# Keys and values ahead of the queries in a two-layer graph network kernel, with two smaller moves

## The chip, the cores and the metric

The kernel runs on one core of a Trainium2 chip. The metric is the device time of one execution in microseconds, lower is better.

## The reference

A graph of 3125 nodes with 128 features and 103125 edges (sources `src`, targets `dst`, sorted by target). Cut to what matters:

```python
# layer 0: graph convolution
deg  = segment_sum(1, src);  norm = rsqrt(deg)[src] * rsqrt(deg)[dst]
x = layernorm(x + segment_sum(norm * (x @ weight)[src], dst) + bias)
# layer 1: message passing with edge weights from two small networks
w = silu(edge64 @ rad_w0 + rad_b0) @ rad_w1 + rad_b1
w = w + silu(edge32 @ sph_w0 + sph_b0) @ sph_w1 + sph_b1
q = (x @ wq)[dst];  k = (x @ wk)[src];  v = (x @ wv)[src]
alpha = (q * w * k).sum(per head of 16) / sqrt(16) * edge_weight
x = layernorm(x + segment_sum(alpha * v, dst) / 16)
```

## The kernel before, in words

The edges are cut into 202 groups of 512 (four tiles of 128). Each engine has its own program, written by hand, and all order between engines comes from semaphores that the code names. Four stages follow one another.

**Prologue.** VectorE counts degrees with one-hot rows, scales the node rows (L1211), splits the first layer's weights of the edge networks into a high and a low part (L1218, L1222), then checks with two reductions (L1227, L1228) that the sorted order of the targets fits the windows. The checked values come from GpSimd: differences (L620, L624 to L635), then a copy and two scalings (L639 to L641), counted on the semaphore `s_set`. From the check follow the two pass counts, one for each sweep; every engine reads them from SBUF into a register (L416), and each is 1 for these inputs. TensorE waits for the split weights through `s_pre` (L916).

**Sweep one** runs over all groups: GpSimd gathers scaled node rows for half of them, the others are counted into dense blocks, TensorE sums both into `acc` (a column for each node) and also computes the edge weights of a quarter of the groups, which are stored to HBM.

**The gap.** 25 blocks of 128 nodes go in 7 chunks of 4 (the last has one). For a chunk c, in this order of engines: TensorE multiplies `acc` with the layer's weights (`convolve`, L1032); VectorE adds the rows, takes statistics; ScalarE takes the root (`root`, L815) and normalises (`scaled`, L821); TensorE transposes (L1042); ScalarE copies the transposes to `x_t`, two chunk buffers (`copy_transposes`, L829); `project` on TensorE makes queries (L1051), then keys and values (L1058). ScalarE copies keys and values out (`copy_kv`, L849) and, with VectorE, splits the queries into three bf16 parts: `q_hi` (L836), the rest (L1445), `q_mid` (L841), the low part (L1448). `q_rest` is one buffer, `q_parts` has four chunk slots, reused when the stores of the chunk four earlier have landed (L835). All of that is one software pipeline, with one loop on each engine. SyncE's loop (L531 to L543) stores a chunk's keys and values (L534), then waits for its low part and stores three query parts (L538; for chunk 1 three more, L542), then takes the next chunk. GpSimd adds a bias to the node rows (L691), clears `acc` (L694), and waits until all keys and values have landed (L696).

**Sweep two** runs over all 202 groups, in 50 steps of four and a last one of two. GpSimd issues four indirect gathers of keys and values for each group (L657, a ring of eight group slots, reused after the message of the group eight earlier). SyncE loads the gather's indices (L461, after the gathers of four pairs before have landed, L460), rows, queries (L506, the first only after all query stores, L552), edge features (L451, L453) and stored weights. ScalarE and VectorE split features, TensorE runs the edge network (L930, L932, L948), expands queries (L1082) and sums messages (L958). VectorE multiplies keys with queries (L1487), then with weights (L1499), sums heads (L1504), makes the message (L1519), in an order written out by hand in `sweep2`. At the end the second layer norm and the stores to `out`.

Of the kernel before, what the change touches and what calls it, by code (L numbers as in the profile page):

```python
# [19 lines left out]
P = 128  # L20
# [114 lines left out]
def build(nc, x, x_pad, src_idx, src_e, dst_e, dst_row, dst_first, cut_e, rad_t, sph_t, w_l0, b_l0, rad_w0, rad_b0,  # L135
# [24 lines left out]
    with ExitStack() as ctx:  # L160
# [132 lines left out]
        x_t, to = part(count, 0, 2 * CHUNK * P)  # L293
        x_t = x_t.rearrange("p (k f) -> p k f", k=2)
        q_rest, to = part(count, to, CHUNK * D)
# [139 lines left out]
        def _(sp):  # L435
# [95 lines left out]
            for c in range(CHUNKS):  # L531
# [3 lines left out]
                             kv_out[:, c % 4, 0:n, :]).then_inc(s_kvt[c % 4], 16)  # L535
                sp.wait_ge(s_lo, c + 1)
# [53 lines left out]
        def _(pool):  # L590
# [56 lines left out]
            assert v == SET.all, v  # L647

            pool.wait_ge(s_pre, PRE.passes)
            n_pass1, n_pass2 = passes(pool, 1), passes(pool, 2)  # L650
# [38 lines left out]
            for c in range(CHUNKS):  # L689
                own = nodes[:, blocks(c)[0]:blocks(c)[-1] + 1, :]  # L690
                pool.tensor_tensor(own, own, b_l0_sb[:, :].unsqueeze(1).to_broadcast([P, len(blocks(c)), D]),  # L691
                                   ALU.add).then_inc(s_biased, 1)
            pool.wait_ge(s_conv, CHUNKS)
# [10 lines left out]
        def _(act):  # L704
# [44 lines left out]
            n_pass1, n_pass2 = passes(act, 1), passes(act, 2)  # L749
# [74 lines left out]
            def copy_transposes(c):  # L824
                act.wait_ge(s_tr, c + 1)
                if c >= 2:
                    act.wait_ge(s_proj, blocks(c - 2)[-1] + 1)
                cols = slice(0, len(blocks(c)) * P)
                act.activation(x_t[:, c % 2, cols], bank[2 + c % 2][:, cols], ACT.Copy).then_inc(s_trc, 1)  # L829
# [8 lines left out]
            def q_mid(c):  # L838
                cols = slice(0, len(blocks(c)) * D)
                act.wait_ge(s_rest, c + 1)  # L840
                act.activation(q_parts[:, c % 4, 1, cols], q_rest[:, cols], ACT.Copy).then_inc(s_mid, 1)  # L841
# [25 lines left out]

# [8 lines left out]

            with act.Fori(0, n_pass2) as p:
# [12 lines left out]
        def _(pe):  # L890
# [25 lines left out]
            pe.wait_ge(s_pre, PRE.w0)  # L916
# [128 lines left out]
            def project(c):  # L1045
                pe.wait_ge(s_trc, c + 1)
                if c >= 2:
                    pe.wait_ge(s_rest, c - 1)
                for b in blocks(c):
                    at = b % CHUNK * P  # L1050
                    mm = pe.matmul(bank[4 + c % 2][:, at:at + D], x_t[:, c % 2, at:at + P], wqkv[:, 0:D],  # L1051
                                   start=True, stop=True, skip_group_check=True)
                mm.then_inc(s_projq, 1)
                for b in blocks(c):
                    if b >= 4 and b % 2 == 0:
                        pe.wait_ge(s_projc, b // 2 - 1)
                    at, to = b % CHUNK * P, b % 2 * 2 * D
                    pe.matmul(bank[6 + b // 2 % 2][:, to:to + 2 * D], x_t[:, c % 2, at:at + P], wqkv[:, D:3 * D],  # L1058
                              start=True, stop=True, skip_group_check=True).then_inc(s_proj, 1)
# [3 lines left out]
            for c in range(CHUNKS):  # L1063
# [81 lines left out]
        def _(dve):  # L1145
# [99 lines left out]
            dve.wait_ge(s_set, SET.all)  # L1245
# [193 lines left out]
            def split_q(c):  # L1439
# [3 lines left out]
                if c >= 1:  # L1443
                    dve.wait_ge(s_lo, c)
                dve.tensor_tensor(q_rest[:, cols], bank[4 + c % 2][:, cols], q_parts[:, c % 4, 0, cols],  # L1445
                                  ALU.subtract).then_inc(s_rest, 1)
# [248 lines left out]
```

## Time and profile before

| | us |
|---|---|
| median of 3 runs | 1775.34 (1770.6 to 1778.68) |
| the profiled execution's own time | 1772.56 |
| its span in the profile | 1770.7 |
| TensorE busy | 1571.4 (89%) |
| VectorE busy | 1379.2 (78%) |
| GpSimd busy | 1298.8 (73%) |
| ScalarE busy | 924.5 (52%) |

Sweep one begins at about 84 us of the span and ends at about 621; the gap reaches to 667, sweep two to about 1748. Busy shares are averages over these stages, so a change in one stage has to be read in the rows of that stage. PE is TensorE, DVE is VectorE, ACT is ScalarE, POOL is GpSimd, SP is SyncE; a q behind the name is the engine's queue, which also issues DMAs.

### The profile page before, as it was taken

To read this page: it belongs to the slowest core of one execution; us is meant where nothing else is said; L and a number is where in the kernel's file an instruction comes from. 1 tells how busy PE (TensorE), PEld (TensorE's weight loads), DVE (VectorE), ACT (ScalarE), POOL (GpSimd) and SP (SyncE) were. 2 spreads that over 40 slices of the span, in tenths; PEclk is the share of its full clock that TensorE was granted. 3 is DMA by queue.
4 is the path that set the end of the run, shared out by engine and by line. 5 is a ranking of instruction groups with operands and counts; after the bars stand their busy time and mean duration, and the time that the engine had idled before them with its cause. 6 is when DMAs were issued, how large, how long until landed. Compare 5 with 4: busy or idle time off the path is not lost.

```text
span 1770.7 us, 45707 instructions
## 1 busy us (share of the span) xinstructions
PE 1571.4 (89%) x12986; PEld 1454.2 (82%) x12986; DVE 1379.2 (78%) x3869; ACT 924.5 (52%) x1399; POOL 1298.8 (73%) x1249
## 2 busy tenths in 40 slices
PE   3389999899899978999999999999999999999995
PEld 2278888888888866889988898989898898888984
DVE  8986777777777566887887788887888777888886
ACT  1144555554555374555555555555555555555563
POOL 8777777777777627777777777777777777777771
PEclk9999999999999988999999999999999999999997
DMA  3133333333333266666666666666666666666663
GB/s 100 43 104 101 107 105 99 106 105 99 106 105 100 77 166 160 178 177 175 181 178 172 175 174 176 179 176 184 178 176 179 177 175 172 172 178 176 180 181 105
DMA packets 177657, 259.26 MB, mean 146 GB/s; under 512 B 80694, under 2 KB 91757, under 8 KB 177436
## 3 DMA queue, kind: packets, MB, share of 16 engines
q0 software_dynamic: 51840, 132.72, 27.8%
q1 hardware_dynamic: 120008, 120.99, 24.4%
q10 hardware_dynamic: 5716, 4.55, 0.9%
q8 instruction: 30, 0.49, 0.1%
q14 instruction: 63, 0.52, 0.1%
HBM read 235.32 MB, written 22.79 MB: 146 GB/s over the span
## 4 chain that ended last, share of the span: by engine, by line
POOL 43%; issue 18%; DVE 14%; PE 14%; DVEq 4%; DMA 3%; POOLq 1%; SPq 1%; ACT 1%; ACTq 1%
POOL arena L657 40%; PE bank L948 5%; PE bank L991 4%; DVE count L1342 4%; POOL rel L620 3%; DVE xsplit L1309 2%; DVE key_hot L1330 2%; PE bank L958 2%; DVE low_hot L1329 2%; DVEq L1315 1%; DMA arena<-kv_d,idx 1%; DMA xraw<-in_sph_t 1%; DVEq L1342 1%; PE bank L930 1%; POOLq L674 1%
## 5 line engine op out<-in xcount | busy, mean ns | idle before, releaser
L657 POOL DMA_INDIRECT arena<-kv_d,idx x808 | 823.3, 1019 | 264.4 <-issue 262.3
L948 PEld LDWEIGHTS bank<-w,hid 128*128 128x128 f32 x6464 | 779.9, 193 | 24.0 <-ACT hid L773 1.5
L948 PE MATMUL bank<-w,hid 128*128 128x128 f32 x6464 | 788.7, 277 | 0.0
L773 ACT ACTIVATE hid<-bank,b 128x512 f32<-128x512 f32 x808 | 495.6, 683 | 308.3 <-PE bank L932 301.7
L657 POOL DMA_INDIRECT arena<-xs_d,idx x408 | 394.5, 967 | 139.8 <-issue 121.0
L930 PE MATMUL bank<-xsplit,w_hi 128*128 128x512 f32 x808 | 344.8, 437 | 79.1 <-ACT hid L773 54.5
L765 ACT ACTIVATE xsplit<-xraw 64x1024 fp32r<-64x1024 f32 x202 | 212.4, 1052 | 239.0 <-DMA xraw<-in_sph_t 224.1
L1309 DVE TENSOR_TENSOR xsplit<-xraw,xsplit 64x256 fp32r<-64x256 f32 x808 | 287.9, 413 | 6.6 <-ACT xsplit L765 0.2
L930 PEld LDWEIGHTS bank<-xsplit,w_hi 128*128 128x128 f32 x808 | 154.7, 191 | 113.2 <-ACT hid L773 63.4
L1342 DVE TENSOR_TENSOR count<-count,bank 128x200 f32 x400 | 144.5, 361 | 124.8 <-issue 57.9
L958 PE MATMUL bank<-onehot,late 128*128 128x126 f32 x1616 | 215.0, 281 | 6.3 <-DVE late L1519 4.5
L958 PEld LDWEIGHTS bank<-onehot,late 128*128 128x128 f32 x1616 | 193.2, 192 | 8.6 <-DVE late L1519 6.4
L1478 DVE TENSOR_SCALAR late<-late,iota_part 126x512 bf16<-126x512 bf16 x202 | 73.6, 365 | 118.8 <-PE bank L1082 102.6
L932 PE MATMUL bank<-xsplit,w_lo 128*128 128x512 f32 x404 | 160.4, 397 | 0.0
L1487 DVE TENSOR_TENSOR late<-arena,bank 128x512 f32<-128x512 f32 x202 | 137.3, 680 | 14.2 <-DMA arena<-kv_d,idx 10.2
L1499 DVE TENSOR_TENSOR late<-late,bank 128x512 f32<-128x512 f32 x151 | 102.9, 681 | 57.9 <-PE bank L948 52.8
L1519 DVE TENSOR_TENSOR late<-arena,alpha 128x512 f32<-128x512 f32 x202 | 138.6, 686 | 3.6 <-DVE alpha L1511 1.5
L1504 DVE TENSOR_REDUCE red<-late 128x32 f32<-128x512 f32 x202 | 136.8, 677 | 0.0
L791 ACT ACTIVATE w_sb<-bank 128x512 f32<-128x512 f32 x51 | 30.5, 597 | 189.6 <-PE bank L948 189.4
L757 ACT ACTIVATE bank<-b_full 128x512 f32<-128x512 f32 x199 | 118.6, 596 | 1.6
L1330 DVE TENSOR_SCALAR key_hot<-iota_key,key 128x200 bf16<-128x200 bf16 x400 | 113.4, 285 | 0.0
L1329 DVE TENSOR_SCALAR low_hot<-iota_key,low_f 128x128 bf16<-128x128 bf16 x400 | 107.6, 270 | 0.2
(144 smaller groups left out, 1310.6 us busy)
## 6 DMA issues: line engine op xcount, KB each, us to landing
late<-relrow_d SPq DMA_DIRECT2D x103, 256.0 KB
xraw<-in_rad_t SPq DMA_DIRECT2D x205, 128.0 KB
xraw<-in_sph_t SPq DMA_DIRECT2D x410, 64.0 KB
w_sb<-w_d SPq DMA_DIRECT2D x52, 256.0 KB, 4.0
w_d<-w_sb SPq DMA_DIRECT2D x51, 256.0 KB
arena<-kv_d,idx POOLq DMA_INDIRECT x808
arena<-xs_d,idx POOLq DMA_INDIRECT x408
qwin<-q_d SPq DMA_DIRECT2D x101, 31.5 KB
```

Of the source, the lines that this page charges most:

```text
L657: pool.indirect_dma_start(gath[:, k, t * width:(t + 1) * width], None, table, bass.IndirectOffsetOnAxis(ap=idx[:, pair.slot(4), j * TILES ...
L765: act.activation(xsplit[0:RAD, s.slot(2), :, :], xraw[:, k, :, :], ACT.Copy).then_inc(mlp.s_hi, 1)
L773: act.activation(hid[:, s.slot(2), c, :], hid_ps[s.sub(4, c, 4 * s.total).slot(len(hid_ps))][:, :], ACT.Silu, bias=b0[:, c:c + 1]).then_in ...
L930: mm = pe.matmul(to, w0_hi[:, m, cols], xsplit[:, b, m, :], start=True, stop=(m == 1))
L932: mm = pe.matmul(to, w0_lo[:, m, cols], xsplit[:, b, m, :], start=False, stop=True)
L948: mm = pe.matmul(w_ps[:, t * D:(t + 1) * D], hid[:, b, c, t * P:(t + 1) * P], w1[:, c, :], start=False, stop=(c == 3), skip_group_check=True)
L958: return pe.matmul(bank[7][:, at:at + 3 * WIN], rows, onehot[:, b, first:first + 3, :].rearrange("p t n -> p (t n)"), start=(k == 0), stop ...
L1309: last = dve.tensor_tensor(xsplit[RAD:P, b, m, half], xraw[:, k, m, half], xsplit[0:RAD, b, m, half].bitcast(F32), ALU.subtract)
L1329: dve.tensor_scalar(low_hot[:, t, :], iota_key[:, 0:LO], low_f[:, ds(col, 1)], None, ALU.is_equal)
L1330: last = dve.tensor_scalar(key_hot[:, t, :], iota_key[:, :], key[:, ds(col, 1)], None, ALU.is_equal)
L1342: dve.tensor_tensor(here, here, count_ps[j % 2][:, t * KEYS:(t + 1) * KEYS].rearrange("p (h w) -> p h w", h=NB), ALU.add).then_inc(s_add, 1)
L1519: dve.tensor_tensor(msg[:, j, :, :].rearrange("p t (h d) -> p t h d", d=HD), kv(g)[:, :, 1, :].rearrange("p t (h d) -> p t h d", d=HD), a, ...
```

## The change

1. The weights' split moves from VectorE (`pre`, counted on `s_pre`) to GpSimd (`step`, counted on `s_set`), behind GpSimd's copies for the spans. TensorE waits for `s_set`.
2. GpSimd and ScalarE read the first sweep's pass count at the old place; the second's only after the bias additions (GpSimd) and right before sweep two (ScalarE).
3. In the gap, the pipeline loop carries keys and values alone, for all chunks. `x_t` now holds all 25 blocks. The queries get a loop of their own behind it, on TensorE, ScalarE, VectorE and SyncE. `q_rest` gets two slots, in the memory of `prod`. SyncE stores all keys and values before any query part. TensorE waits for the last `s_rest` before sweep two.

The three subtractions, the sizes of the stores and every matrix product stay as they were.

```diff
-        x_t, to = part(count, 0, 2 * CHUNK * P)
-        x_t = x_t.rearrange("p (k f) -> p k f", k=2)
-        q_rest, to = part(count, to, CHUNK * D)
+        x_t, to = part(count, 0, NB * P)
+        q_rest = prod
...
                 sp.dma_start(kv_d[rows, :].rearrange("(b p) f -> p b f", p=P),
                              kv_out[:, c % 4, 0:n, :]).then_inc(s_kvt[c % 4], 16)
+
+            for c in range(CHUNKS):
+                n, rows = len(blocks(c)), slice(blocks(c)[0] * P, (blocks(c)[-1] + 1) * P)
                 sp.wait_ge(s_lo, c + 1)
...
-            assert v == SET.all, v
+            assert v == SET.spans, v
+            pool.wait_ge(s_whi, 1)
+            v = step(pool.tensor_tensor(w0_lo[:, :, :], w0_raw[:, :, :], w0_hi[:, :, :].bitcast(F32), ALU.subtract))
+            step_wait(v)
+            for j in (1, 3):
+                own = slice(j * SPH, (j + 1) * SPH)
+                v = step(pool.tensor_tensor(w0_hi[own, 1, :], w0_raw[own, 1, :], w0_hi[own, 1, :].bitcast(F32), ALU.subtract))
+            assert v == SET.w0, v
+            step_wait(v)
 
             pool.wait_ge(s_pre, PRE.passes)
-            n_pass1, n_pass2 = passes(pool, 1), passes(pool, 2)
+            n_pass1 = passes(pool, 1)
...
                                    ALU.add).then_inc(s_biased, 1)
+            n_pass2 = passes(pool, 2)
             pool.wait_ge(s_conv, CHUNKS)
...
-            n_pass1, n_pass2 = passes(act, 1), passes(act, 2)
+            n_pass1 = passes(act, 1)
...
             def copy_transposes(c):
                 act.wait_ge(s_tr, c + 1)
-                if c >= 2:
-                    act.wait_ge(s_proj, blocks(c - 2)[-1] + 1)
...
                 if c < CHUNKS:
                     copy_transposes(c)
-                if c >= 1:
-                    q_hi(c - 1)
                 if c + 1 < CHUNKS:
                     scaled(c + 1, s_shift, s_norm)
                 if c >= 1:
                     copy_kv(c - 1)
-                    q_mid(c - 1)
                 if c + 2 < CHUNKS:
                     root(c + 2, s_var, s_std)
+            for c in range(CHUNKS + 1):
+                if c < CHUNKS:
+                    q_hi(c)
+                if c >= 1:
+                    q_mid(c - 1)
...
+            n_pass2 = passes(act, 2)
             with act.Fori(0, n_pass2) as p:
...
-            pe.wait_ge(s_pre, PRE.w0)
+            pe.wait_ge(s_set, SET.w0)
...
                 if c >= 1:
-                    project(c - 1)
-            project(CHUNKS - 1)
+                    project_kv(c - 1)
+            project_kv(CHUNKS - 1)
+            for c in range(CHUNKS):
+                project_q(c)
             pe.wait_ge(s_projc, (NB + 1) // 2)
+            pe.wait_ge(s_rest, CHUNKS)
...
-            dve.wait_ge(s_whi, 1)
-            v = pre(dve.tensor_tensor(w0_lo[:, :, :], w0_raw[:, :, :], w0_hi[:, :, :].bitcast(F32), ALU.subtract))
-            pre_wait(v)
-            for j in (1, 3):
-                own = slice(j * SPH, (j + 1) * SPH)
-                v = pre(dve.tensor_tensor(w0_hi[own, 1, :], w0_raw[own, 1, :], w0_hi[own, 1, :].bitcast(F32), ALU.subtract))
-            assert v == PRE.w0, v
...
-                if c >= 1:
-                    split_q(c - 1)
+            for c in range(CHUNKS + 1):
+                if c < CHUNKS:
+                    rest_of_q(c)
+                if c >= 1:
+                    low_of_q(c - 1)
```

`project_kv` and `project_q` are the two halves of `project`, and `rest_of_q` and `low_of_q` those of `split_q`, with their waits; `rest_of_q(c)` waits for the low part of chunk c - 2.

## Rows read from the trace of the kernel before

**Rows 1.** The page's costliest groups: busy, mean ns of one | idle before.

```profile
L657 POOL DMA_INDIRECT arena<-kv_d,idx x808 | 823.3, 1019 | 264.4 <-issue 262.3
```

**Rows 2.** Timeline of the gap's end: start us, us, engine, line, operation.

```profile
660.92 0.39 ACT L849 ACTIVATE arena<-bank 128x256 f32<-128x256 f32 x1
...
663.68 0.54 SPq L534 DMA_DIRECT2D kv_d<-arena  x1
...
667.38 1.05 POOL L657 DMA_INDIRECT arena<-kv_d,idx  x1 [18.48 <-issue]
```

**Rows 3.** Waits of GpSimd, 700 to 1760 us: total us, times, longest us.

```profile
POOL arena L657 <- issue: 236.5, 776, 0.3
```

**Rows 4.** Waits of SyncE's queue, 700 to 1760 us.

```profile
SPq L460 <- DMA arena<-kv_d,idx: 431.9, 95, 6.3
```

**Rows 5.** Timeline of VectorE in sweep two, first products of two steps.

```profile
808.21 0.68 DVE L1487 TENSOR_TENSOR late<-arena,bank 128x512 f32<-128x512 f32 x1
...
828.11 0.68 DVE L1487 TENSOR_TENSOR late<-arena,bank 128x512 f32<-128x512 f32 x1
```

**Rows 6.** Windows of sweep two: PE, PEld, DVE, ACT, POOL busy (instructions), PEclk, DMA, GB/s.

```profile
700.00:900.00 200.00, 189.47 (x1535) 179.54 (x1532) 164.51 (x384) 111.24 (x170) 153.93 (x152) 0.99 0.66 179
...
760.00:780.00 20.00, 20.00 (x166) 19.03 (x165) 17.34 (x41) 12.01 (x20) 15.43 (x16) 1.00 0.64 169
```

**Rows 7.** Timeline of ScalarE in the gap.

```profile
639.74 0.59 ACT L829 ACTIVATE count<-bank 128x512 f32<-128x512 f32 x1
...
640.21 0.60 ACT L836 ACTIVATE count<-bank 128x512 bf16<-128x512 f32 x1
...
643.77 0.63 ACT L841 ACTIVATE count<-count 128x512 bf16<-128x512 f32 x1 [0.37 <-DVE count L1445]
...
658.03 0.27 ACT L829 ACTIVATE count<-bank 128x128 f32<-128x128 f32 x1
```

**Rows 8.** Timeline of TensorE in the gap.

```profile
641.61 1.05 PE L1032 MATMUL bank<-w_l_sb,acc 128*128 128x128 f32 x8
...
642.94 1.06 PE L1051 MATMUL bank<-wqkv,count 128*128 128x128 f32 x8
...
643.83 1.89 PE L1058 MATMUL bank<-wqkv,count 128*128 128x256 f32 x8
```

**Rows 9.** Timeline of VectorE: a query subtraction, first product, first message.

```profile
643.05 0.69 DVE L1445 TENSOR_TENSOR count<-bank,count 128x512 f32<-128x512 f32 x1
...
674.15 0.69 DVE L1487 TENSOR_TENSOR late<-arena,bank 128x512 f32<-128x512 f32 x1 [6.57 <-DMA arena<-kv_d,idx]
...
680.92 0.69 DVE L1519 TENSOR_TENSOR late<-arena,alpha 128x512 f32<-128x512 f32 x1
```

**Rows 10.** The query stores' line: issue ns min/median/max, first and last start.

```profile
L538 SPq DMA_DIRECT2D q_d<-count x21: 372/454/989, 640.5 to 665.2; - x21
```

**Rows 11.** DMA view, 655 to 672 us: GB/s in 40 slices; stores, KB, us to landing.

```profile
GB/s 301 318 225 211 214 217 28 0 202 347 316 343 224 206 216 222 298 347 311 324 236 214 215 215 300 227 97 0 0 0 0 0 55 175 154 11 213 180 0 193
...
kv_d<-arena SPq DMA_DIRECT2D x2, 512.0 KB, 3.3
```

**Rows 12.** Timeline of the prologue, and TensorE's first layer.

```profile
19.68 51.54 POOL L620 TENSOR_TENSOR rel<-dst_f,base_f 128x808 f32<-128x808 f32 x1 [7.65 <-ACT dst_f L725]
...
71.19 1.02 POOL L624 TENSOR_TENSOR near<-dst_f,tile_f 128x400 f32<-128x400 f32 x1
...
75.16 2.07 POOL L640 TENSOR_SCALAR arena<-near 128x400 f32<-128x400 f32 x1
76.08 1.00 DVE L1218 TENSOR_TENSOR w_lo<-w_raw,w_hi 128x512 fp32r<-128x512 f32 x1
...
77.31 1.29 POOL L641 TENSOR_SCALAR arena<-coff 128x400 f32<-128x400 f32 x1
...
95.33 0.79 PE L930 MATMUL bank<-xsplit,w_hi 128*128 128x512 f32 x1 [12.12 <-DVE xsplit L1309]
```

**Rows 13.** The pass count's read on GpSimd's queue: ns min/median/max.

```profile
L416 POOLq TENSOR_LOAD <-passes_i x2: 312/410/507, 83.7 to 84.5; - x2
```

More of the change, by code:

```diff
@@ L825, in copy_transposes @@
                 act.wait_ge(s_tr, c + 1)
-                if c >= 2:
-                    act.wait_ge(s_proj, blocks(c - 2)[-1] + 1)
                 cols = slice(0, len(blocks(c)) * P)
-                act.activation(x_t[:, c % 2, cols], bank[2 + c % 2][:, cols], ACT.Copy).then_inc(s_trc, 1)
+                own = slice(blocks(c)[0] * P, (blocks(c)[-1] + 1) * P)
+                act.activation(x_t[:, own], bank[2 + c % 2][:, cols], ACT.Copy).then_inc(s_trc, 1)
             def q_hi(c):
@@ L840, in q_mid @@
                 act.wait_ge(s_rest, c + 1)
-                act.activation(q_parts[:, c % 4, 1, cols], q_rest[:, cols], ACT.Copy).then_inc(s_mid, 1)
+                act.activation(q_parts[:, c % 4, 1, cols], q_rest[:, c % 2, cols], ACT.Copy).then_inc(s_mid, 1)
             def copy_kv(c):
@@ L1043, in transpose, with project_kv, project_q @@
                 mm.then_inc(s_tr, 1)
-            def project(c):
+            def project_kv(c):
                 pe.wait_ge(s_trc, c + 1)
+                for b in blocks(c):
+                    if b >= 4 and b % 2 == 0:
+                        pe.wait_ge(s_projc, b // 2 - 1)
+                    to = b % 2 * 2 * D
+                    pe.matmul(bank[6 + b // 2 % 2][:, to:to + 2 * D], x_t[:, b * P:(b + 1) * P], wqkv[:, D:3 * D],
+                              start=True, stop=True, skip_group_check=True).then_inc(s_proj, 1)
+            def project_q(c):
                 if c >= 2:
@@ L1050, in project @@
                     at = b % CHUNK * P
-                    mm = pe.matmul(bank[4 + c % 2][:, at:at + D], x_t[:, c % 2, at:at + P], wqkv[:, 0:D],
+                    mm = pe.matmul(bank[4 + c % 2][:, at:at + D], x_t[:, b * P:(b + 1) * P], wqkv[:, 0:D],
                                    start=True, stop=True, skip_group_check=True)
                 mm.then_inc(s_projq, 1)
[L1054 to L1059, printed above, removed]
             convolve(0)
@@ L1242, in _ @@
             assert v == PRE.passes, v
-            dve.wait_ge(s_set, SET.all)
+            dve.wait_ge(s_set, SET.spans)
             dve.wait_ge(s_cast, CAST.all)
@@ L1437, in scale_and_shift, with rest_of_q, low_of_q @@
                                          op0=ALU.mult, op1=ALU.mult).then_inc(s_shift, 1)
-            def split_q(c):
+            def rest_of_q(c):
                 cols = slice(0, len(blocks(c)) * D)
                 dve.wait_ge(s_hi, c + 1)
-                if c >= 1:
-                    dve.wait_ge(s_lo, c)
-                dve.tensor_tensor(q_rest[:, cols], bank[4 + c % 2][:, cols], q_parts[:, c % 4, 0, cols],
+                if c >= 2:
+                    dve.wait_ge(s_lo, c - 1)
+                dve.tensor_tensor(q_rest[:, c % 2, cols], bank[4 + c % 2][:, cols], q_parts[:, c % 4, 0, cols],
                                   ALU.subtract).then_inc(s_rest, 1)
+            def low_of_q(c):
+                cols = slice(0, len(blocks(c)) * D)
                 dve.wait_ge(s_mid, c + 1)
-                dve.tensor_tensor(q_parts[:, c % 4, 2, cols], q_rest[:, cols], q_parts[:, c % 4, 1, cols],
+                dve.tensor_tensor(q_parts[:, c % 4, 2, cols], q_rest[:, c % 2, cols], q_parts[:, c % 4, 1, cols],
                                   ALU.subtract).then_inc(s_lo, 1)
@@ L1625 @@
     xs = 14
-    w0 = 18
-    viol = 22
-    passes = 25
+    viol = 19
+    passes = 22
 class SET:
     rel = 8
-    all = 11
+    spans = 11
+    w0 = 14
 class CAST:
```

## The prediction

> **What bounds the kernel now.** I read the page's costliest groups first, looking for the instruction that fills an engine without a gap. It is GpSimd's second gather: 808 of them, 1.019 us each, with 264.4 us of idle in front that is nearly all "issue" [rows 1]. 18.48 of that lies ahead of the first one, at 667.38 [rows 2]; the rest is (264.4 - 18.5) / 807 = 0.305 apiece. So a gather takes 1.019 + 0.305 = 1.324 us and a step of four groups (16 gathers) 21.2. GpSimd's waits over the second sweep say that no gap was longer than 0.3 us: it never waited for anybody [rows 3]. So the end moves with the **start of the first gather**, as long as the others keep up.
>
> Do the others follow GpSimd or set its pace? SyncE's waits tell: 95 of its index loads, of one for each of 101 pairs, stood until a gather had landed [rows 4], and the features that feed TensorE are queued behind them. When the others fall behind they make it up: two first products of a step (L1487) stand at 808.21 and 828.11, a step of 19.9 us [rows 5]. The windows show TensorE busy 20.00 of 20 us with 166 instructions done, against 1535 in 200 us on average [rows 6]. A step holds 1535 / 200 x 21.2 = 163 of them, so it can run in 163 / 166 x 20 = 19.6 us. TensorE looks full and has over 1 us in each step to give.
>
> **The gap between the sweeps** (622 to 667). ScalarE's copies of transposes (L829) stand at 639.74 for chunk 2 and 658.03 for chunk 6: a turn is 18.29 / 4 = 4.57 us, and the one idle of a turn is 0.37 [rows 7]. ScalarE sets this loop. Two items of its turn, 0.60 (L836) and 0.63 (L841), serve the queries alone. On TensorE a turn has a convolution of 1.05, four transposes (half its instructions, 0.53), 1.06 of queries and 1.89 of keys and values [rows 8]: 4.53.
>
> **Keys and values first.** Without the queries ScalarE's turn is 4.57 - 1.23 = 3.34 us and TensorE's 4.53 - 1.06 = 3.47; VectorE loses two subtractions of 0.69 [rows 9]. I take 3.5. Copy 2 comes at 638.7, 1 us sooner than now, since scaling no longer waits for a query product; copies 3 to 5 follow at 3.5 each, 649.2. The tail has no convolution left: chunk 4's and 5's keys and values and those of chunk 6's single block (1.89 + 1.89 + 0.5 on TensorE, their copies beside and behind, with the last transposes between) put the last copy's end at 654.9. Now it is 660.92 + 0.39 = 661.31 [rows 2].
>
> SyncE's queue counts too. The last store of keys and values was ready at 661.31 and issued at 663.68, behind query stores [rows 2]: 2.4 us. In the new order only chunk 5's store stands ahead. Issue at 655.2, 8.5 us sooner. The first gather began 3.7 us after that issue [rows 2]. The 512 KB store right before it needs 3.3 to land [rows 11], so I give back 0.5: first gather at 659.4, **8.0 us sooner**. Ends: 5 (the three engines wait for one another, a turn near 4.2) and 10 (a turn of 3.2, since operations overlap a little).
>
> **Queries in a loop of their own.** They start when ScalarE has copied the last keys, 654.9, and end later than now. Per chunk ScalarE does 0.60 + 0.63 and VectorE 0.69 + 0.69 [rows 7, 9]; seven chunks at 1.4 give 665. But a part buffer comes free only when the stores of the chunk four earlier have landed, and SyncE issues 24 stores (21, and 3 for the rows past the end) at 0.45 each [rows 10], 11 us, from 657.8 on: 669, some 3 more to land, 672. Their data runs at 201 to 234 GB/s where keys and values reach 302 to 350 [rows 11]: 2.4 MB in 11 us, and the gathers (131 KB each 1.32 us) want a third of that time, up to 677. The last query store is now issued at 665.2 [rows 10] and is in by 668. So the queries are 4 to 9 us late, and the first product of sweep two, which at 674.15 still waited 6.57 for its gather [rows 9], comes at 674 to 679. **Priced at nothing**: the cover is the distance between a gather and its use. A slot is gathered again eight groups (42.4 us) on; the first message ended at 681.6 [rows 9], at most 687 afterwards, and is needed by 659.4 + 42.4 = 701.8. The lag of up to 5 + 8 = 13 us is worked off at 21.2 - 19.9 = 1.3 us a step, in ten of the fifty. Without that cover it costs the lateness itself, 0 to 5 us.
>
> **Weights on GpSimd.** VectorE's L1218 (1.00) and both L1222 go. VectorE then waited for GpSimd's L641, which ended at 78.60, so their own time is worth nothing. What counts is that GpSimd's two scalings ran beside them, 2.07 and 1.29 us, though L624 over the same 400 columns took 1.02 [rows 12]. At 1.02 each they end 1.3 sooner; part of L640 stands beside L1211, which stays, so I take **1.0 us sooner**, ends 0 and 1.8. VectorE's chain from there to the sweep carries it whole. The Trainium skill (SBUF — State Buffer, "Who interferes with whom") says that a VectorE operation with two SBUF inputs and a GpSimd one that reads SBUF shut each other out for the whole instruction, and that a VectorE reduction never does; L640 did end 0.15 after L1218, so the trace agrees. By that rule the estimate would be 1.8. The three subtractions cost GpSimd 512 x 2.55 ns + 2 x 0.65 = 2.6 us (2.55 ns a column, from L624), 78.3 to 81; TensorE needs them at 94, one before its 95.33 [rows 12], and GpSimd's next work is the first gather. Nothing.
>
> **Pass count read later.** A read is a load of 0.3 to 0.5 us on each engine's queue and some 0.2 after it [rows 13]. GpSimd's moves beside VectorE's statistics, at 630: nothing. ScalarE's moves in front of sweep two, +0.65, where the work waits for queries: nothing.
>
> **Sum**, against the profiled execution's 1772.56: -8.0 - 1.0 = 1763.6. It lies 2.8 us under the median of the runs shown, 1775.34; there the sum is **1766.3**, -0.51%. A measurement of this kernel tells about 0.5% (8.9 us) from no change, so the forecast stands on that line.
>
> **Rivals.**
> Half the gain (11%): the engines of the new loop wait for one another, a turn of 4.5; first gather 4 us sooner, -5, 1770.3. For it: three turns of nearly equal length. Against: ScalarE idles only 0.37 in a turn.
> The first weights held back (4%): GpSimd's L620 took 51.54 us for 808 columns while VectorE made 16-bit one-hots [rows 12]. If the new subtractions are held so until about 101, TensorE's first layer (95.33) starts 5.7 late: -8 + 5.7, 1773. Against: L640 and L641 got through beside VectorE.
> **Slower** (12%, of it 5% past the line): the queries decide. Place: first product of sweep two. If steps can't run under 21.2 us, the end moves with that product and not with the gather. At 679 that is +5 - 1, 1779; if buffers and shared transfers push it to 689, +15 - 1, 1789. It decides once the lag outlives the 50 steps, 13 / 50 = 0.26 a step, so at steps over 20.9. Against it: the 19.9 of [rows 5].
> More than forecast (8%): a turn of 3.2, nothing given back, 1.8 in front: -12, 1763.3.
>
> **Numbers.** The forecast has 65%; its spread of some 2 us either way and that of the runs put 42 of these past the line and 23 within. Faster 42 + 8 = 50%; within 23 + 11 + 4 + 7 = 45%; slower 5%. Range 1760.5 to 1772.5: -12 and -5 with the scatter of a median of runs (they lay 1770.6 to 1778.7) of some 2.5 beyond each.
>
> **What would show it.** L1227 1 us sooner; copies of transposes 3.5 apart; last store of keys and values issued near 655 and the first gather near 659, each less that 1 us; query stores in one block to about 669; first product at 674 to 679, then steps under 20.5 until the lag is back; and still no gap over 0.4 us between gathers. It is wrong if GpSimd waits for VectorE's messages.

## The result, and the profile after

| | before | after |
|---|---|---|
| median of 20 runs each, us | 1773.39 | 1769.15 (1761.77 to 1775.31) |
| ratio, 95% interval | 1 | 0.9971 (0.9958 to 0.9983) |
| the profiled execution, us | 1772.56 | 1775.31 |

The change makes the kernel 0.3% faster, some 5 us by the ratio, where 9 were forecast. The time lies in the range. One of the 20 runs of the kernel before took 2772.29 us; it hardly moves the median. The profiled execution of after is the slowest of its 20 runs. So the totals of the two pages must not be held against each other, and below a stage is read from three executions of the same gap (after, e1 and e10).

The page's costliest group, which answers to [rows 1]:

```profile
L667 POOL DMA_INDIRECT arena<-kv_d,idx x808 | 833.1, 1031 | 260.4 <-issue 257.3
```

The idle in front of the gathers is 4.0 us less than before, all of it at the first gather (14.46 us where it was 18.48). The mean gather is 12 ns longer, which over 808 is 9.8 us: in this execution more than the head start.

The gap between the sweeps, timeline of after (columns as in [rows 2]): ScalarE's copies of transposes (L839), then SyncE's last two stores of keys and values (L533), GpSimd's clear of the accumulator (L705) and the first gather (L667), and one small VectorE operation (L1424).

```profile
637.70 0.60 ACT L839 ACTIVATE count<-bank 128x512 f32<-128x512 f32 x1 [0.34 <-PE bank L1055]
640.78 0.59 ACT L839 ACTIVATE count<-bank 128x512 f32<-128x512 f32 x1
645.79 0.58 ACT L839 ACTIVATE count<-bank 128x512 f32<-128x512 f32 x1
648.92 0.58 ACT L839 ACTIVATE count<-bank 128x512 f32<-128x512 f32 x1
...
654.75 0.91 SPq L533 DMA_DIRECT2D kv_d<-arena  x2
...
642.74 2.88 POOL L705 MEMSET acc<- 128x3344 f32 x1 [13.11 <-PE bank L1045]
660.08 0.97 POOL L667 DMA_INDIRECT arena<-kv_d,idx  x1 [14.46 <-issue]
...
643.50 2.15 DVE L1424 TENSOR_SCALAR rstd<-meanvar 128x4 f32<-128x4 f32 x1
645.68 0.20 ACT L826 ACTIVATE rstd<-rstd 128x4 f32<-128x4 f32 x1 [1.74 <-DVE rstd L1424]
```

A turn is 3.1 us, except one of 5.0: copies at 640.78 and 645.79. VectorE's operation on four columns, elsewhere 0.17, took 2.15 and ended at 645.65, which is 0.03 after the end of GpSimd's clear (642.74 + 2.88 = 645.62). ScalarE's root stood 1.74 for it. The first gather begins 7.3 us sooner than in [rows 2].

The queries and the start of sweep two, timelines of SyncE's queue and VectorE:

```profile
671.86 1.01 SPq L540 DMA_DIRECT2D q_d<-count  x2
676.27 1.78 SPq L505 DMA_DIRECT2D qwin<-q_d  x2
...
679.27 0.69 DVE L1502 TENSOR_TENSOR late<-arena,bank 128x512 f32<-128x512 f32 x1 [4.77 <-PE bank L1100]
```

The last query store goes out at 672.4 and the first query load 3.9 us later. The first product stands 5.1 us after that of [rows 9], and it now waits for the expanded queries and not for its gather.

GpSimd's waits, 700 to 1760 us, and two windows (columns as in [rows 6]):

```profile
POOL arena L667 <- issue: 233.7, 767, 0.3
POOL arena L667 <- DVE late L1534: 3.0, 10, 0.3
```

```profile
660.00:680.00 20.00, 6.37 (x31) 4.39 (x30) 9.33 (x23) 11.60 (x17) 15.35 (x16) 0.64 0.88 216
700.00:900.00 200.00, 195.59 (x1616) 186.66 (x1615) 169.84 (x400) 119.57 (x180) 154.51 (x150) 1.00 0.67 180
```

Still no gap over 0.3 us, as in [rows 3]: GpSimd sets the end in both kernels. The engines behind it do 1616 matrix instructions in 200 us where [rows 6] has 1535, and VectorE is busy 169.84 instead of 164.51: they work the lag off. Their first step of four groups, from first product to first product, takes 27.0 us (26.6 in the kernel before), the next ones 19.5 to 19.7 each.

The prologue, timeline of after, answers to [rows 12]:

```profile
75.17 2.07 POOL L642 TENSOR_SCALAR arena<-near 128x400 f32<-128x400 f32 x1
77.31 1.21 POOL L643 TENSOR_SCALAR arena<-coff 128x400 f32<-128x400 f32 x1
...
78.56 1.83 DVE L1236 TENSOR_REDUCE small<-arena 128x1 f32<-128x1608 f32 x1 [2.40 <-POOL arena L643]
...
78.88 1.25 POOL L651 TENSOR_TENSOR w_lo<-w_raw,w_hi 128x512 fp32r<-128x512 f32 x1
80.21 1.52 POOL L655 TENSOR_TENSOR w_hi<-w_raw,w_hi 32x256 fp32r<-32x256 f32 x2
...
94.94 0.79 PE L943 MATMUL bank<-xsplit,w_hi 128*128 128x512 f32 x1 [11.79 <-DVE xsplit L1318]
```

VectorE's subtraction is gone from beside the two scalings, and they take 2.07 and 1.21 us as before (2.07 and 1.29).

### The profile page after: what moved, and what is told of

Read it like the earlier page. It is cut to its first block, busy times and chain, and to the rows that moved or that the text cites. A ratio compares the mean times of both kernels' runs of the same rounds, so it can differ in the third digit from the quotient of the medians.

```text
span 1773.5 us, 45704 instructions
## 1 busy us (share of the span) xinstructions
PE 1572.9 (89%) x12986; PEld 1456.7 (82%) x12986; DVE 1379.2 (78%) x3866; ACT 926.0 (52%) x1399; POOL 1310.4 (74%) x1252
## 4 chain that ended last, share of the span: by engine, by line
POOL 44%; issue 18%; PE 15%; DVE 14%; DVEq 4%; DMA 2%; POOLq 1%; ACTq 1%; SPq 1%; ACT 1%
POOL arena L667 40%; PE bank L961 5%; PE bank L1004 4%; DVE count L1351 4%; POOL rel L622 3%; DVE xsplit L1318 2%; DVE key_hot L1339 2%; DVE low_hot L1338 2%; PE bank L971 2%; DVEq L1324 1%; PE bank L943 1%; DVEq L1351 1%; POOLq L684 1%; DMA arena<-kv_d,idx 1%; DMA xraw<-in_sph_t 1%
## 5 line engine op out<-in xcount | busy, mean ns | idle before, releaser
L667 POOL DMA_INDIRECT arena<-kv_d,idx x808 | 833.1, 1031 | 260.4 <-issue 257.3
L667 POOL DMA_INDIRECT arena<-xs_d,idx x408 | 394.3, 966 | 136.9 <-issue 121.3
L1318 DVE TENSOR_TENSOR xsplit<-xraw,xsplit 64x256 fp32r<-64x256 f32 x808 | 287.6, 412 | 6.4
L1514 DVE TENSOR_TENSOR late<-late,bank 128x512 f32<-128x512 f32 x151 | 103.1, 683 | 56.3 <-PE bank L961 51.6
L1534 DVE TENSOR_TENSOR late<-arena,alpha 128x512 f32<-128x512 f32 x202 | 138.8, 687 | 3.6 <-DVE alpha L1526 1.9
```

Source lines behind the costliest of these rows:

```text
L667: pool.indirect_dma_start(gath[:, k, t * width:(t + 1) * width], None, table, bass.IndirectOffsetOnAxis(ap=idx[:, pair.slot(4), j * TILES ...
L1318: last = dve.tensor_tensor(xsplit[RAD:P, b, m, half], xraw[:, k, m, half], xsplit[0:RAD, b, m, half].bitcast(F32), ALU.subtract)
L1534: dve.tensor_tensor(msg[:, j, :, :].rearrange("p t (h d) -> p t h d", d=HD), kv(g)[:, :, 1, :].rearrange("p t (h d) -> p t h d", d=HD), a, ...
```

## The experiments

The kernels came in four sessions, each with its own runs of the kernel before (1772.83, 2555.86, 1772.33 and 2489.86 us). In the second and the fourth the granted clock of TensorE was 0.84 and 0.86 on the mean of every execution, instead of 0.98; these numbers are compared with one another alone.

### e1_gap_only and e2_front_only: one part of the change each

e1 is the changed kernel with the weights back on VectorE and both pass counts read early; e2 has those two moves, and the gap of the kernel before. Both cuts are against the changed kernel.

```diff
 e1:
-            n_pass1 = passes(act, 1)
+            n_pass1, n_pass2 = passes(act, 1), passes(act, 2)
...
-            pe.wait_ge(s_set, SET.w0)
+            pe.wait_ge(s_pre, PRE.w0)
 e2:
-                    project_kv(c - 1)
+                    project(c - 1)
```

> Only the gap is reordered (keys and values first, queries in their own loop); weights' split and pass counts as in the kernel before. Theory A (the end moves with the first gather, and the gap gave all of the gain): first gather near 660.4, last store of keys and values issued near 656, time 5 to 7 us under the kernel before. Rival (the front moves matter as I forecast, 1.0 us or more of the gain): at most 4 us under the kernel before.

> Only the weights' split on GpSimd and the later pass counts. Theory A: VectorE's first reduction starts only 0.1 us sooner because GpSimd's scaling there takes as long as before; TensorE's first layer 0.4 sooner; time 0 to 0.5 us under the kernel before, not to be told from no change. Rival (my forecast): 1.0 us or more sooner, first reduction at 77.6.

Measured: e1 1768.89 us, ratio 0.9983 (0.9966 to 0.9999), first gather at 659.43; e2 1772.70 us, ratio 0.9998 (0.9982 to 1.0013), first gather at 667.00, first reduction of the check at 78.55 (78.63 in the kernel before). So the gap's part carries the gain, and the two moves in front show none: 0.1 us by the medians of e2, and no difference within its interval. The gain of e1, 3.9 by the medians, is less than the 5 to 7 that its first theory gave and lies where its rival had it (at most 4), but the rival's reason, a gain in front, is what e2 does not show. In e2 the first layer of TensorE starts 0.41 us sooner (94.92 against 95.33 of [rows 12]).

### e3_gather_held: the first gather behind the query stores

The changed kernel, with one wait more on GpSimd ahead of the gathers:

```diff
+            for j in range(4):
+                pool.wait_ge(s_qt[j], 48 * (chunks_in(j, 4) + (j == 1)))
```

> The changed kernel, but GpSimd also waits until all query stores have landed before its first gather of sweep two. Theory A (the end follows the first gather one to one): first gather near 677, 17 us later than in the changed kernel, end 17 us later, about 12 us slower than the kernel before. Theory B (the first product decides and gathers are hidden): no more than 4 us over the changed kernel. Theory C (working off the lag makes gathers longer, about 4 us of the early start given back): end only 13 us later than in the changed kernel, because there is no lag to work off, with the gather stream back to about 1068 us.

Measured: 1779.35 us, ratio 1.0036 (1.0021 to 1.0051).

```profile
674.75 0.97 POOL L667 DMA_INDIRECT arena<-kv_d,idx  x1 [28.00 <-issue]
...
681.42 0.69 DVE L1504 TENSOR_TENSOR late<-arena,bank 128x512 f32<-128x512 f32 x1 [7.22 <-DMA arena<-kv_d,idx]
```

The first gather is 14.7 us later than in after, the first product only 2.2, and the median is 10.2 higher (10.5 above e1's, which stands beside the same runs of before). If the first product decided, it would be 2. So the end follows the gather. But nearly a third of the 14.7 did not arrive: these 4.5 us were owed to something that a late start doesn't have, as the third theory had it. Against e2, which starts late too, the gather is 7.75 us later and the median 6.7 higher. The gathers themselves tell where the rest went. GpSimd's groups by line, for gathers 65 to 128 (the second block of 64) of before, after and e3: busy, mean ns | idle before.

```profile
L657 POOL DMA_INDIRECT arena<-kv_d,idx x64 | 65.3, 1021 | 19.5 <-issue 19.5
```

```profile
L667 POOL DMA_INDIRECT arena<-kv_d,idx x62 | 66.3, 1069 | 18.9 <-issue 18.6 <-DVE late L1534 0.3
```

```profile
L667 POOL DMA_INDIRECT arena<-kv_d,idx x65 | 66.0, 1016 | 19.8 <-issue 19.5 <-DVE late L1536 0.3
```

And the windows of the same stretches, in the same order:

```profile
751.00:835.00 84.00, 78.64 (x634) 74.89 (x635) 66.89 (x158) 47.16 (x72) 64.71 (x64) 0.98 0.64 178
```

```profile
743.00:828.00 85.00, 85.00 (x708) 81.41 (x707) 72.84 (x170) 51.63 (x78) 66.15 (x62) 1.00 0.67 180
```

```profile
758.00:843.00 85.00, 76.65 (x618) 72.81 (x617) 64.48 (x151) 46.91 (x72) 65.23 (x65) 0.98 0.66 179
```

Where the others catch up, VectorE is busy 86% of the stretch instead of 80 and 76, and a gather takes 1.069 us instead of 1.021 and 1.016. In e1, e10 and e4, which start early too, it takes 1.065, 1.069 and 1.073; in e2, which starts late, 1.010. That is 0.05 us times 64, 3 us given back, in each of the kernels with the early start and in no other. Over the first 128 gathers together it is 2.4 us, since the first 64 are a little shorter in most of the early ones (0.995 in after, 1.012 in before). Single blocks of 64 reach 1.05 later on without a lag (in e2 and e3), so one trace would not show this; it is the agreement of all of them that does. Which of VectorE's operations the gathers meet is told under e8.

### e4_clear_late: the clear of the accumulator out of VectorE's way

```diff
+            pool.wait_ge(s_shift, CHUNKS)
```

stands ahead of GpSimd's clear (L705) in the changed kernel: it waits until VectorE is through with its small operations.

> The changed kernel, but GpSimd clears the accumulator only after VectorE's last shift. In the changed kernel one VectorE operation of 4 columns took 2.15 us beside that clearing, and ScalarE idled 1.74 behind it; TensorE then ran its last products slowly. Theory A: copy 4 of transposes comes at 644.1 instead of 645.8, first gather 1.7 to 3 us sooner than 660.1, time 2 to 3 us under the changed kernel. Rival (keys' last store waits for something else, or the clearing only moves the stall to another VectorE operation): first gather within 0.5 us of 660.1.

Measured: 1764.97 us, ratio 0.9956 (0.9940 to 0.9972). The medians of this kernel and e1 stand beside the same runs of before, and this one is 3.9 lower (the two intervals overlap a little). Its gap, by the timeline of ScalarE and GpSimd:

```profile
641.16 0.59 ACT L840 ACTIVATE count<-bank 128x512 f32<-128x512 f32 x1
644.31 0.58 ACT L840 ACTIVATE count<-bank 128x512 f32<-128x512 f32 x1
647.45 0.58 ACT L840 ACTIVATE count<-bank 128x512 f32<-128x512 f32 x1
...
648.07 2.88 POOL L706 MEMSET acc<- 128x3344 f32 x1 [18.76 <-DVE shift L1446]
656.12 0.97 POOL L667 DMA_INDIRECT arena<-kv_d,idx  x1 [5.17 <-issue]
```

The turn of 5.0 us is gone (641.16, 644.31, 647.45), and the first gather begins at 656.12, 4.0 sooner than in after. This version is clearly faster than the kernel before, and by the medians faster than the changed one.

Not all of the 4 us is the held operation. The windows 650 to 652 us of after and of e10, which is the same kernel (columns as in [rows 6]):

```profile
650.00:652.00 2.00, 2.00 (x6) 1.55 (x5) 0.00 (x0) 0.60 (x1) 0.00 (x0) 0.50 0.70 241
```

```profile
650.00:652.00 2.00, 2.00 (x10) 1.44 (x8) 0.00 (x0) 1.39 (x4) 0.00 (x0) 1.00 0.64 217
```

TensorE's granted clock stood at 0.50 (1.2 GHz) in after while it ran the last products, and at 1.00 (2.4 GHz) in e10; it fell there in e1, e3, e8 and e9 too, and not in e4. Just before, from 644 to 648, TensorE had been busy 2.52 of 4 us in after, 2.48 in e10 and 3.69 in e4, so the held operation left it idle in the first two, and what made the clock fall in one and not in the other these rows don't tell. From GpSimd's first bias addition to its first gather it is 38.25 us in after, 37.90 in e1, 36.12 in e10 and 34.61 in e4. So at the full clock the later clear is worth 1.5 us (36.12 - 34.61); the other 2.1 of the 3.6 is the clock.

### e5_msg_one_input, e6_q_twice, e7_changed_again: a session with a lower clock

e5 is the changed kernel with VectorE's message made from one input (the edit is shown under e8, which repeats it), e6 issues every query store twice (shown under e9), e7 is the changed kernel itself.

> The changed kernel, but VectorE writes the message with a reduction over an axis of one, one SBUF input instead of two; the multiplication by the attention weight is left out, so the message is the bare value row. Theory L (a gather that meets a VectorE operation with two SBUF inputs waits for it): gathers beside the message fall from 1.12 to about 0.98, the mean of all from 1.03 to about 0.995, the stream from 1070 to 1078 down to 1045 or less, the time 25 to 30 us under the changed kernel. Rival (long gathers come from DMA load or from the gather itself): mean stays at 1.02 to 1.03 and the time within 4 us of the changed kernel.

> The changed kernel with each query store issued twice, the second to a table that nothing reads, so that the queries are some 10 us later. Theory A with C (the first product's lateness costs nothing by itself, working it off lengthens some gathers): first product near 689, first gather still near 660, no gap between gathers over 0.4 us, four or five more steps at 19.5, time 0 to 4 us over the changed kernel. Theory B (the first product decides): 10 us over it. If the ring runs out, GpSimd waits for VectorE's message for more than 0.4 us somewhere in the first 100 us, and the time is 5 us or more over.

> The changed kernel once more. Theory C (the lag's cost is systematic, gathers 65 to 128 long): their mean is 1.06 to 1.07 again, as in the three early-start profiles, where the three profiles without a lag had 1.01 to 1.02; time 4 to 5 us under the kernel before. Rival (that stretch was chance): their mean falls at 1.02 like the others.

Measured: e5 2598.66 us, ratio 1.0162 (1.0125 to 1.0199); e6 2553.04, 0.9991 (0.9968 to 1.0014); e7 2548.60, 0.9975 (0.9950 to 0.9999). None of them can tell the theories apart, since GpSimd is not the bound there. (e5 and e8 leave out the multiplication by the attention weight, so their messages are bare value rows.) The page of e7:

```profile
PEclk9988888888888868888888888888888888887887
...
L667 POOL DMA_INDIRECT arena<-kv_d,idx x808 | 802.8, 994 | 795.2 <-DVE late L1534 559.8
```

The gathers wait 559.8 us for VectorE's messages, behind a TensorE whose granted clock falls to half again and again: 0.84 on the mean, where before and after have 0.98. A gather that waits for others also takes less itself, 994 ns against 1031. That e5 is slower by 1.6% is not explained; its executions had a granted clock of 0.836 on the mean and the others 0.844.

### e8_msg_one_input_b: what makes a gather long

```diff
-                dve.tensor_tensor(msg[:, j, :, :].rearrange("p t (h d) -> p t h d", d=HD),
-                                  kv(g)[:, :, 1, :].rearrange("p t (h d) -> p t h d", d=HD), a,
-                                  ALU.mult).then_inc(s_msg, 1)
+                dve.tensor_reduce(msg[:, j, :, :].rearrange("p t (f o) -> p t f o", o=1),
+                                  kv(g)[:, :, 1, :].rearrange("p t (f o) -> p t f o", o=1), AX.X, ALU.add).then_inc(s_msg, 1)
```

> The message with one SBUF input once more, now hoping for a chip that grants TensorE its full clock most of the time (the first try ran at a mean clock of 0.84, where GpSimd waited for VectorE and the question could not be read). Theory L: mean gather about 0.995 us, stream 1045 us or less, time 25 to 30 us under the changed kernel. Rival: mean 1.02 to 1.03, time within 4 us. A third way: the gathers shorten but TensorE's steps of 19.5 us or VectorE hold the end, so that only 5 to 20 us come.

Measured: 1738.02 us, ratio 0.9806 (0.9780 to 0.9833). The page, GpSimd's gathers and the exchanged operation:

```profile
L667 POOL DMA_INDIRECT arena<-kv_d,idx x808 | 796.9, 986 | 260.4 <-issue 257.4
L1534 DVE TENSOR_REDUCE late<-arena 128x512 f32<-128x512 f32 x202 | 137.5, 680 | 3.6 <-DVE alpha L1526 2.1
```

In after the same operation with two inputs in SBUF takes VectorE 138.8 us, 687 ns each: VectorE's own work is as long as before. What changed are the gathers, 986 ns instead of 1024 in e10, the changed kernel beside it (1031 in after), with nearly the same idle in front (260.4 and 258.8). 38 ns times 808 is 31 us, and the median fell by 32 against e10, somewhat more than the 25 to 30 of the theory. One gather of e8 is longer than 1.3 us; the kernels with the multiplication have 43 to 55.

The trace of after says more exactly what makes a gather long. Timelines of VectorE and GpSimd, in pairs, an operation and the gather that begins inside it: the message, a product with stored weights, the head sums.

```profile
771.30 0.69 DVE L1534 TENSOR_TENSOR late<-arena,alpha 128x512 f32<-128x512 f32 x1
771.36 1.45 POOL L667 DMA_INDIRECT arena<-kv_d,idx  x1 [0.30 <-issue]
...
681.71 0.69 DVE L1514 TENSOR_TENSOR late<-late,w_sb 128x512 f32<-128x512 f32 x1
681.87 1.35 POOL L667 DMA_INDIRECT arena<-kv_d,idx  x1 [0.30 <-issue]
...
758.71 0.68 DVE L1519 TENSOR_REDUCE red<-late 128x32 f32<-128x512 f32 x1
758.92 0.95 POOL L667 DMA_INDIRECT arena<-kv_d,idx  x1 [0.30 <-issue]
```

The first two gathers end 0.82 us after the operation (772.81 against 771.99, 683.22 against 682.40). The same holds all over sweep two: 300 gathers of after begin inside an operation with two SBUF inputs (the message, the features' split L1318, the one-hot rows L1311, the product with stored weights) that has more than 0.15 us to go, and each ends 0.80 to 0.84 us after it. A gather that begins first, or inside the head sums (a reduction) or a product that reads PSUM, takes 0.95. L1514 is one line with and without a PSUM input, and its gathers differ, so it is the inputs and not the kind of operation. The length of a gather is set by how much of such an operation is left when it begins. Counted over 0.95, those that begin inside a message lose 35 us in after and 32 in e10, and this is what e8 took away.

It also says what happens while the others catch up. Of gathers 65 to 128, 11 begin inside a message in after and 10 in before, but they lose 4.4 us and not 2.5. Steps of 19.5 us follow one another there, and the gathers repeat with them: at 769.60, 789.12 and 808.63 one begins 0.04 to 0.05 us after a message, takes 1.45 or 1.46, and the next one does so again. So the price is less that VectorE is fuller than where in the message the gathers fall.

### e9_q_twice_b: the queries later still

```diff
-                    sp.dma_start(q_d[rows, part, :].rearrange("(b p) f -> p b f", p=P),
-                                 q_parts[:, c % 4, part, 0:n * D].rearrange("p (b f) -> p b f", f=D)
-                                 ).then_inc(s_qt[c % 4], 16)
+                    for rows_of in (q_d, q_twice):
+                        sp.dma_start(rows_of[rows, part, :].rearrange("(b p) f -> p b f", p=P),
+                                     q_parts[:, c % 4, part, 0:n * D].rearrange("p (b f) -> p b f", f=D)
+                                     ).then_inc(s_qt[c % 4], 16)
```

> Query stores issued twice, at the full clock. Theory A with C: first product near 689, first gather near 660, no gap over 0.4 us between gathers, time 0 to 4 us over the changed kernel. Theory B: 10 us over it.

Measured: 1780.08 us, ratio 1.0040 (1.0024 to 1.0055). The timeline of VectorE's first product and of three gathers, and GpSimd's waits from 700 to 1760:

```profile
693.47 0.69 DVE L1504 TENSOR_TENSOR late<-arena,bank 128x512 f32<-128x512 f32 x1 [11.14 <-PE bank L1102]
...
710.48 1.16 POOL L669 DMA_INDIRECT arena<-kv_d,idx  x1 [4.08 <-DVE late L1536]
717.10 1.16 POOL L669 DMA_INDIRECT arena<-kv_d,idx  x1 [1.71 <-DVE late L1536]
727.07 1.00 POOL L669 DMA_INDIRECT arena<-kv_d,idx  x1 [5.05 <-DVE late L1536]
```

```profile
POOL arena L669 <- DVE late L1536: 13.0, 10, 5.0
```

The first product is 14.2 us later than in after. The time is what the rival gave, in which the first product decides, and the forecast of no gap over 0.4 us failed. Now GpSimd waits: for the messages of groups 1, 2 and 3 before it may fill their slots again, 4.08 + 1.71 + 5.05 less the usual 0.30 each, 9.9 us. The median is 9.9 above e10's of the same session. So the edge is there, and past it lateness costs about one to one; the agreement to a tenth is luck, since the first gather of this trace is also 2.3 us later than e10's. Where the changed kernel stands from that edge, two timelines of after show, VectorE's message of group 3 and the gather that fills its slot again:

```profile
710.89 0.69 DVE L1534 TENSOR_TENSOR late<-arena,alpha 128x512 f32<-128x512 f32 x1
...
716.89 1.08 POOL L667 DMA_INDIRECT arena<-kv_d,idx  x1 [0.30 <-issue]
```

5.3 us are left (716.89 - 711.58), and 14.2 - 5.3 = 8.9 is about what GpSimd waited in e9. For group 0 it is 15: message at 685.57, gather at 701.33.

### e10_changed_c: the changed kernel again

No edit; it stands beside e8 and e9.

> The changed kernel once more, at the full clock. Theory C: gathers 65 to 128 at a mean of 1.06 to 1.07 us again, as in the three early-start profiles, against 1.01 to 1.02 in the three without a lag. Rival (chance): near 1.02.

Measured: 1770.21 us, ratio 0.9991 (0.9976 to 1.0006), first gather at 658.10, last at 1730.51. Gathers 65 to 128 take 1.065 us on the mean, as the first theory had it. Against the runs of before beside it the gain is 1.6 us by the ratio, with no difference within the interval; in the first comparison it was 5.1 (3.0 us at the least), and e1 had 3.0.

### e11_q_some_twice and e12_before_clear_late: again at a lower clock

e11 is e9 with only the stores of chunks 4 to 6 doubled; e12 is the kernel before with e4's line.

> The changed kernel with the query stores of chunks 4 to 6 alone issued a second time, into a copy that nobody reads: nine more stores of 0.45 us on SyncE's queue, so the queries come about 4 to 5 us later than in the changed kernel (with all 21 stores doubled they came 14 us later, and GpSimd waited 10 us in all for the messages of groups 1 to 3). Theory A, GpSimd's stream sets the end and the queries cost nothing until a slot of the ring is not free in time: first gather as in the changed kernel (within 1 us), first product of sweep two near 684, the smallest distance between a message and the gather that reuses its slot (message 3) falls from 5.3 us to about 1, no gap between gathers over 0.5 us, and the median stays within 2 us of the changed kernel's. Theory B, the first product decides: the median rises by the product's lateness, 4 to 5 us.

> The kernel before with one edit: GpSimd clears the first layer's accumulator only when VectorE is through with all chunks' shifts. Theory A, what the clear cost in the changed kernel (4 us) comes from where it fell there, on the small operations of VectorE that the shorter turns leave no room around: in the kernel before, turns are 4.6 us and the queries set ScalarE's turn, so at most 1 us is won and the first gather starts at 666.4 to 667.4. Theory B, the clear costs the same 3 to 4 us in both kernels, so that the two edits are independent: first gather at 663 to 664, and the median 3 to 4 us under that of the kernel before.

Measured: e11 2487.59 us, ratio 0.9989 (0.9969 to 1.0009); e12 2489.16, ratio 1.0000 (0.9979 to 1.0021). The clock was low again and GpSimd waited for messages 520.1 and 513.1 us, so e11 says nothing of the edge (its longest wait for a message there, 9.0 us, is TensorE's lateness and stands in e12 too), and neither median says what the clear is worth. The gap of e12 can be read with some care: from the bias additions to the first gather it is 38.28 us in e7 and 38.25 in after, though 36.12 in e10. The timeline of e12's GpSimd:

```profile
847.37 7.80 POOL L691 TENSOR_TENSOR nodes<-nodes,b_l_sb 128x512 f32<-128x512 f32 x7 [18.42 <-DVE acc L1324]
879.04 2.89 POOL L695 MEMSET acc<- 128x3344 f32 x1 [23.87 <-DVE shift L1437]
890.56 0.97 POOL L657 DMA_INDIRECT arena<-kv_d,idx  x1 [8.63 <-issue]
```

890.56 - 847.37 = 43.2 us, against 667.38 - 622.14 = 45.2 in the kernel before: 2.0 us, between the two expectations. The clear was no harmless part of the old gap either; in the new one the later clear saved 3.6 us (38.25 - 34.61, by e4's 621.51 and 656.12). In both the granted clock has a part: in the kernel before it fell to 0.50 at 654 to 656 us, inside the gap, in e12 it stood at 1.00 until the last store. No run parts the two there. The clear's own share is in the timeline of VectorE in the kernel before, beside the clear of 646.01 to 648.90:

```profile
647.61 1.31 DVE L1415 TENSOR_SCALAR rstd<-meanvar 128x4 f32<-128x4 f32 x1
```

It too was held to the clear's end (648.92), but for 1.1 us of its own, since it came later in the clear, and in turns of 4.6 us.

## Why the prediction was right, and where it was not

**The bound: right.** The end follows GpSimd's gathers (e3), which wait for nobody in after. The rival in which the queries decide does not hold at a first product of 679.27, nor at e3's 681.42; at 693 it does, by the ring's slots and not by the first product as such (e9).

**The gap, -8.0: right.** The first gather began at 660.08, in e1 at 659.43 and in e10 at 658.10, against 667.38 before and 667.00 in e2: 8.0 us on the mean, forecast 659.4. Counted from the first bias addition, so without the scatter in front, it is 7.7, and 7.0 where the clock fell (45.23 in before, 38.25 in after). Its steps: the last store went out near 655.2 as forecast, the first gather followed 4.8 us later (3.7 before, so 1.1 were given back where I had 0.5), and chunk 5's copy stood at 648.92 (forecast 649.2). That agreement hides two errors of opposite sign. A turn is 3.1 us and not 3.5, and one of them is 5.0, because of the clear beside VectorE's statistics. I had passed over the clear as work of an idle engine. Of the "half the gain" rival the number is near and the mechanism is not: there is no turn of 4.5 us.

**The queries, "priced at nothing": the step that failed.** The first product came at the end of my range (679.27). The last query store was issued at 672.4 and not at 669: the 24 stores stood 0.6 us apart and not 0.45. All were in by 676.3, when the first load went out, and GpSimd kept its cover. But catching up is not free. In its steps of 19.5 us the gathers begin inside VectorE's two-input operations at dearer places: 64 gathers are longer by 0.05 us, 3 us (e3, e8). With 8.0 us sooner and 3 back, the mean gain is 5; by the ratios it is 5.1, 3.0 and 1.6 us in after, e1 and e10, on the mean 3.2. The other 2 us lie within what the runs scatter and aren't assigned: from first to last gather these three take 1078.1, 1074.2 and 1072.4 us, and before, e2 and e3 1068.3, 1071.4 and 1070.9. I also looked for the edge at the wrong slot. Message 0 had 15 us left, as worked out, but the first step of four groups takes 27 us and not 19.9, as it did in the kernel before (26.6), and message 3 has only 5.3. A price of nothing was right for this lateness, by luck as to its margin.

**The weights, -1.0: wrong.** Worth 0.1 us at the place where I put the gain (the first reduction at 78.56, in the kernel before at 78.63), and 0.4 at TensorE's first layer, in which the later read of the second pass count may have its part (no run took the two apart); e2 shows no time for both. The step that failed is "at 1.02 each they end 1.3 sooner". The second scaling takes 1.21 us in after with no VectorE operation beside it: that is its own length, not the 1.02 of L624. The first still takes 2.07; beside it lies only the scaling of the node rows, L1211 before and L1229 now, which ended at 76.16, 1.1 us before the scaling's end in both kernels. So if anything holds it, it is the operation that stays; no run took that one away. The gathers speak for it: they end 0.82 us after such an operation and take 0.95 by themselves, 0.13 more, and this scaling ends 1.08 after it and would take 1.21, again 0.13 more. That L640 ended 0.15 after VectorE's subtraction, which I had called agreement, was chance. The Trainium skill (SBUF — State Buffer, "Who interferes with whom") would have given 1.8 us here; the run shows 0.1. It is not the rule that this speaks against, but my laying it on L1218: with L1211 in its place there is nothing to win. The three subtractions cost GpSimd 2.85 us, forecast 2.6, and nobody waited for them.

**The pass count, nothing:** as forecast, within the 0.4 us above.

**The sum:** -9.0 forecast; -8.0 at the first gather, nothing in front, about +3 back in the catching up. That the time lies in the range owes something to its width: two of the terms, the catching up and the weights, were mis-sized by 4 us together.

## What to carry to other kernels

Where one engine issues without a gap, move its start, and count what the others do while they catch up: if they share something with it, the lag has a price even when no wait shows. Ask of each of its instructions what runs beside it at the moment it begins. Check a ring's cover at every slot of the first ragged steps and not at the first one alone. And look at the long single operations of an engine that seems idle (here a clear of 2.9 us): beside another engine's chain of short ones they can cost half a turn, and in some executions TensorE's clock fell behind it; one wait moved the clear away, for 1.5 us at the full clock and 3.6 otherwise.

## What the runs showed of the hardware that was not expected

**A gather's length depends on VectorE's operands.** A gather takes 0.95 us; where it begins inside a VectorE operation with two SBUF inputs it ends 0.82 us after that operation, up to 1.46 us in all (300 gathers of after); inside a reduction, or where it begins first, it takes 0.95. With the message made a reduction the kernel is 32 us faster (e8 against e10). The Trainium skill (SBUF — State Buffer, "Who interferes with whom") says that a reduction never contends, and the runs agree; it infers that a two-input operation doesn't hold up GpSimd's making of descriptors, and e8 speaks against that.

**A short operation held to the end of a clear.** A VectorE operation on four columns ended 0.02 us (before) and 0.03 us (after) after GpSimd's clear, 1.31 and 2.15 us long instead of 0.17; with the clear moved away it took 0.17 in e4 and in e12. The same section says that such an operation can need the pair of ports that both engines share, and that the one who is second waits for the whole instruction; the traces agree, and e4 shows the price together with the clock's.

**A granted clock that is low for a whole session.** Eight tenths instead of nearly ten made the same kernel 2490 to 2556 us long, with GpSimd no longer the bound. One of the sessions was on the chip that had given 1772.83 before, so it is no property of a chip. What caused it stays open.
